# Four-layer graph network on one core: TensorE transposes the identity 6 to 20 times ahead of four of its waits

## The chip, the cores and the metric

One core of one Trainium2 chip runs the whole program. The metric is the device time of one execution in microseconds (us), and less is better. The program has five instruction streams that meet only at semaphores: TensorE (PE in the profile, PEld for its weight loads), VectorE (DVE), ScalarE (ACT), GpSimd (POOL) and SyncE (SP).

## The reference, cut to what matters

Sixteen graphs (batches) of 512 nodes with 256 features, each with its own 512x512 adjacency, go through four layers. After each layer the result is added to its input and normalized.

```python
x = _layernorm(x + _L0_gnn_ref(x, adj, ...))   # graph attention, one head, ELU
x = _layernorm(x + _L1_gnn_ref(x, adj, ...))   # three blocks: attention, layernorm, feed-forward 256-1024-256, layernorm
x = _layernorm(x + _L2_gnn_ref(x, adj, ...))   # graph attention that keeps the 16 largest weights of a row, ELU
x = _layernorm(x + _L3_gnn_ref(x, adj, ...))   # eight heads, relu, output projection
# one block of layer 1
scores = leaky(si[:, :, None] + sj[:, None, :] + attn_b[l]); attn = softmax(where(mask, scores, -inf))
h = layernorm(x + attn @ x, g1[l], beta1[l])
x = layernorm(h + gelu(h @ W1[l] + b1[l]) @ W2[l] + b2[l], g2[l], beta2[l])
```

Batches don't depend on each other. Everything is computed in float32.

## The kernel before

All weights stay in SBUF. Two batches are under way at any time, one in each of two slots with buffers of their own, half a batch apart: while one slot does the middle of its batch (layers L0, L1.0, L1.1 and the attention of L1.2), the other does the end of the batch before (the feed-forward of L1.2, then L2 and L3). The table HALF (line 56 on) is a hand-written order of named stages for one such pass, and every engine walks the same table, in the same order, doing its own part of each stage. A pass with one slot in the middle and a pass with the other in the middle alternate: an opening, seven turns of a loop of two passes, and a closing, so that each stage below runs 16 times in the program.

So an engine never overtakes within its own stream: if TensorE waits in a stage, all that stands behind it in HALF waits as well, whichever slot it belongs to.

PSUM has eight banks, four for each slot: `work` banks 0 and 1, which the slot's stages use in turn, and `acc` banks 0 and 1, in which the aggregations, the feed-forward's second product and the projections accumulate. The class `Use` (line 336) gives for the n-th use of a stage its bank, and the count that the bank's `evacuated` semaphore must have reached for the bank to be free. One stage's tile is in bank i % 2 of a running number i, so the tile after two transposed tiles takes the bank of the first of the two.

A stage's name has the layer beside it. Those around the change, as TensorE does them:

- `xT0`, `xT1`: wait until half of the rows is normalized (VectorE, line 732), and transpose it in two work tiles of two 128x128 transposes (line 1067). ScalarE copies the first tile to XT (line 911, for the h of the blocks line 972), VectorE the second (line 630, for h line 775).
- `v0` of L2 (line 1097): waits for both copies, then multiplies the half with the weights, in two work tiles.
- `s` and `bc` of L1.0 (lines 1110, 1126): attention scores of every node, 16 matmuls of two columns, and the spread of one of them by transposes.
- `pT0` to `pT3` (line 1138): wait for the exponential of a row tile, transpose the weights; `agg0`, `agg1` (line 1152): wait for the copies of the transposed weights (ScalarE line 950, VectorE line 711) and multiply them with the features.
- `hT0`, then `f100` (line 1174): the first feed-forward product of the first half, which waits for both copies of hT0's tiles; `f101` to `f103` are the rest of it, and `f200` (line 1188) begins the second product.

The wait in `f100` and what follows are these lines:

```python
if quarter == 0:
    for c in range(DC):
        u = Use(s, it, f"hT{half} {key}", c)
        pe.wait_ge(u.evacuated, u.turn + 1)
for f in range(quarter * FQ, (quarter + 1) * FQ):
    u = Use(s, it, f"g{half} {key}", f)
    pe.wait_ge(u.evacuated, u.turn)
```

In HALF the pieces stand so: `L1.2 f210 f211`, `L2 xT0`, `L0 norm1`, `L2 v0`, `L1.0 xT1 s bc`, `L1.2 f212 f213`, `L1.0 zs0 mx0 zs1 exp0 mx1 exp1 pT0`, `L1.0 pT1`, `L1.0 agg0`, `L1.0 pT2 pT3`, `L2 xT1 v1 bc`, `L2 zs0 mx0`, `L1.0 agg1`, `L2 zs1 exp0`, `L1.0 hT0 ha0 sum1 norm1 f100 f101 hT1 ha1`. In this list ScalarE has the exponentials (`exp0` of L2) ahead of its copy for `hT0`.

Of the kernel before, what the change touches and what calls it, by code (L numbers as in the profile page):

```python
# [12 lines left out]
P = 128  # L13
# [44 lines left out]
def build(nc, x, adj, w0, a01, a02, attn_w, attn_b, w1, b1, w2, b2, g1, beta1, g2, beta2,  # L58
# [81 lines left out]
    ]  # L140

    def half_batch(middle, other, after, ending=True, starting=True):
# [14 lines left out]
    with ExitStack() as ctx:  # L157
# [897 lines left out]
        def _(pe):  # L1055
            pe.wait_ge(consts, N_CONSTS)

            def wait_weights(key):
                pe.wait_ge(loaded[key], 16 * N_LOADS[key])
                pe.wait_ge(folded[key], N_FOLDED[key])  # L1060

            def transpose_tiles(s, it, key, src, row_tiles):
                for c in range(DC):
                    u = Use(s, it, key, c)
                    pe.wait_ge(u.evacuated, u.turn)
                    for i, t in enumerate(row_tiles):
                        last = pe.transpose(u.bank[:, i * P:(i + 1) * P], src[:, t, c * P:(c + 1) * P], ident[:])  # L1067
                    last.then_inc(u.filled, 1)

            def xT(half):  # L1070
                def stage(s, it, key):
                    if key == "L0":
                        pe.wait_ge(x_in.sems[s], x_in.value(it, "L0", 15))
                        transpose_tiles(s, it, "xT L0", HX[s], range(NT))
                    elif key in L1K[1:]:
                        pe.wait_ge(normed.sems[s], normed.value(it, L1K[L1K.index(key) - 1] + " x", half))
                        transpose_tiles(s, it, f"xT{half} {key}", HX[s], tiles(half))
                    else:
                        pe.wait_ge(normed.sems[s], normed.value(it, MADE_BY[key], half))
                        transpose_tiles(s, it, f"xT{half} {key}", X1[s], tiles(half))  # L1080
                return stage
# [6 lines left out]
            def project_v(half):  # L1088
                def stage(s, it, key):
                    weights, columns = {"L0": (w0_sb, DA), "L2": (wg_sb, DA), "L3": (wv_sb, D)}[key]  # L1090
                    if key != "L0" or half == 0:
                        wait_transposed(s, it, key, half)
                    for t in tiles(half):
# [35 lines left out]
            def weights_transposed(t):  # L1129
                def stage(s, it, key):  # L1130
                    if key == "L2":
                        pe.wait_ge(kept.sems[s], kept.value(it, key, t))
                    else:
                        pe.wait_ge(exp_done.sems[s], exp_done.value(it, key, t))
                    u = Use(s, it, f"pT {key}", t)
                    pe.wait_ge(u.evacuated, u.turn)
                    for j in range(NT):
# [4 lines left out]
            def agg(half):  # L1142
                def stage(s, it, key):
                    pe.wait_ge(acc_evacuated[half].sems[s], acc_evacuated[half].value(it, key) - 1)
                    src = SOURCE[key] if key in L1K else V
                    if key in L1K[1:] and half == 0:
# [10 lines left out]
            def h_transposed(half):  # L1157
                def stage(s, it, key):
                    pe.wait_ge(normed.sems[s], normed.value(it, key + " h", half))
                    transpose_tiles(s, it, f"hT{half} {key}", HX[s], tiles(half))  # L1160
                return stage

            def ffn1(half, quarter):
                def stage(s, it, key):
                    l = L1K.index(key)
                    if quarter == 0:
                        for c in range(DC):
                            u = Use(s, it, f"hT{half} {key}", c)
                            pe.wait_ge(u.evacuated, u.turn + 1)
# [157 lines left out]
```

## Time and profile before

| | before |
|---|---|
| median of 3 runs | 3887.73 us (3886.62 to 3899.89) |
| the profiled execution | 3898.82 us |
| its span, first to last instruction | 3896.9 us |
| mean granted TensorE clock | 0.946 of full |
| PE busy | 3453.9 us, 89% of the span, 18816 matmuls |
| DVE, ACT, POOL busy | 2408.7, 2204.8, 695.6 us (62%, 57%, 18%) |

Busy is the time in which an engine has an instruction in it; matmuls are pipelined, so that their starts lie closer than one lasts. The granted clock is the share of TensorE's 2.4 GHz that the chip let through: it has two levels, 1.00 (2.4 GHz) and 0.50 (1.2 GHz), and values between them are means over a stretch. An idle time has behind it the instruction whose end released it.

### The profile page before, as it was taken

The page shows a single profiled execution, that of the slowest core. Times are in us where ns is not written, and L with a number is a line of the kernel's source. Part 1 is how long each engine was busy: PE and PEld are TensorE (multiplying, and loading weights), DVE is VectorE, ACT ScalarE, POOL GpSimd, SP SyncE. Part 2 cuts the span into 40 slices and gives each one's busy share as a digit, 9 for nine tenths or more (in the row PEclk, how much of TensorE's full clock was granted, in tenths as well). Part 3 has the DMA queues.
Part 4 walks back from the last instruction along what each step waited for, and adds up shares of the span by engine and source line. Part 5 has one row for each costly group of instructions (what it writes and reads, how often), then busy time and mean ns, then how long its engine had stood idle before and what let it go on. Part 6 is the DMA issues. An engine that isn't in the chain of part 4 may idle for free.

```text
span 3896.9 us, 60670 instructions
## 1 busy us (share of the span) xinstructions
PE 3453.9 (89%) x18816; PEld 2690.3 (69%) x18816; DVE 2408.7 (62%) x6661; ACT 2204.8 (57%) x4383; POOL 695.6 (18%) x684
## 2 busy tenths in 40 slices
PE   6789989898998989989898898989989899898976
PEld 5667767767777677777777677677767777677653
DVE  3366676666657566676666756566666666766554
ACT  2256556565564746556575564746646565565633
POOL 1211121121212111121121211112121121211110
PEclk8799999999999999999999999999999999999988
DMA  5000000000000000000000000000000000000000
GB/s 129 0 1 12 7 12 7 6 6 6 12 7 6 6 6 12 7 12 6 1 12 7 12 7 6 7 7 12 6 12 7 1 12 6 12 7 1 1 6 6
DMA packets 42354, 39.73 MB, mean 10 GB/s; under 512 B 10017, under 2 KB 40993, under 8 KB 42017
## 3 DMA queue, kind: packets, MB, share of 16 engines
q1 hardware_dynamic: 33568, 27.17, 2.4%
q0 software_dynamic: 8448, 8.39, 1.5%
q8 instruction: 172, 2.82, 0.3%
q14 instruction: 166, 1.35, 0.1%
HBM read 35.55 MB, written 8.39 MB: 11 GB/s over the span
## 4 chain that ended last, share of the span: by engine, by line
PE 48%; issue 33%; DVE 8%; ACT 5%; POOL 5%; DVEq 0%; DMA 0%; POOLq 0%; ACTq 0%; SPq 0%
PE acc L1188 7%; PE work L1174 7%; PE acc L1152 6%; PE work L1097 4%; PE acc L1223 4%; PE acc L1254 3%; POOL rstd L503 3%; PE acc L1235 3%; PE work L1203 2%; PE acc L1283 2%; PE work L1067 2%; PE work L1110 2%; ACT PT L1000 2%; PE work L1235 2%; PE work L1138 1%
## 5 line engine op out<-in xcount | busy, mean ns | idle before, releaser
L1174 PE MATMUL work<-XT,w_sb 128*128 128x256 f32 x3072 | 740.6, 389 | 79.6 <-ACT XT L972 60.9
L503 POOL TENSOR_TENSOR rstd<-var_eps,minus_half 128x2 f32<-128x2 f32 x320 | 233.5, 730 | 3027.9 <-DVE var_eps L727 3027.9
L1188 PE MATMUL acc<-w_sb,gT 128*128 128x256 f32 x3072 | 741.3, 389 | 0.0
L1174 PEld LDWEIGHTS work<-XT,w_sb 128*128 128x128 f32 x3072 | 565.6, 192 | 215.5 <-issue 60.1
L1188 PEld LDWEIGHTS acc<-w_sb,gT 128*128 128x128 f32 x3072 | 588.4, 196 | 101.2 <-issue 22.8
L982 ACT ACTIVATE gT<-work,b_sb 128x256 f32<-128x256 f32 x768 | 346.4, 473 | 227.0 <-PE work L1174 222.5
L1152 PE MATMUL acc<-X,PT 128*128 128x256 f32 x1536 | 359.8, 388 | 32.0 <-ACT PT L950 31.3
L1152 PEld LDWEIGHTS acc<-X,PT 128*128 128x128 f32 x1536 | 292.1, 194 | 86.9 <-issue 48.5
L711 DVE COPY PT<-work 128x512 f32<-128x512 f32 x160 | 110.2, 688 | 237.4 <-PE work L1138 234.7
L718 DVE BATCH_NORM_STATS2 stats<-R 128x6 f32<-128x256 f32 x640 | 240.9, 418 | 11.0
L1152 PE MATMUL acc<-V,PT 128*128 128x256 f32 x1024 | 234.7, 382 | 4.0 <-ACT PT L950 3.8
L982 ACT ACT_TABLE_LOAD x183 | 234.8, 1283 | 3.2
L920 ACT ACTIVATE V<-work 128x258 f32<-128x258 f32 (+1 forms) x192 | 74.1, 386 | 282.5 <-PE work L1097 282.5
L651 DVE CUSTOM_DVE_ANT_0 T<-T,pos 128x512 f32<-128x512 f32 x256 | 178.8, 735 | 63.1 <-ACT T L928 63.1
L658 DVE SCALAR_TENSOR_TENSOR T<-T 128x512 f32<-128x512 f32 x320 | 217.2, 684 | 0.0
L1152 PEld LDWEIGHTS acc<-V,PT 128*128 128x128 f32 x1024 | 192.8, 191 | 31.6 <-issue 4.6
L942 ACT ACTIVATE T<-T,neg_max 128x512 f32<-128x512 f32 x256 | 182.2, 713 | 55.2 <-DVE neg_max L663 51.4
L950 ACT ACTIVATE PT<-work 128x512 f32<-128x512 f32 x160 | 94.7, 592 | 207.7 <-PE work L1138 207.7
L1138 PE MATMUL work<-ident,T 128*128 128x128 f32 x1280 | 176.8, 278 | 31.2 <-ACT T L942 18.4
L928 ACT ACTIVATE T<-work,s 128x512 f32<-128x512 f32 x192 | 117.9, 688 | 144.5 <-PE work L1126 144.5
L1138 PEld LDWEIGHTS work<-ident,T 128*128 128x128 f32 x1280 | 152.7, 143 | 62.5 <-ACT T L942 25.0
L1000 ACT ACTIVATE PT<-PT,head_min 128x512 f32<-128x512 f32 x256 | 182.7, 715 | 0.5
(146 smaller groups left out, 6015.0 us busy)
## 6 DMA issues: line engine op xcount, KB each, us to landing
HX<-in_x SPq DMA_DIRECT2D x16, 512.0 KB, 3.9
pos<-in_adj POOLq DMA_DIRECT2D x16, 512.0 KB, 5.5
out<-X SPq DMA_DIRECT2D x32, 256.0 KB, 2.1
w_sb<-in_L_gnn_W SPq DMA_DIRECT2D x6, 1024.0 KB, 7.9
g_sb<-in_L_gnn_g SPq DMA_DIRECT2D x6, 128.0 KB, 4.7
c_sb<-in_L_gnn_beta SPq DMA_DIRECT2D x3, 128.0 KB, 4.3
PT<-in_L_gnn_b SPq DMA_DIRECT2D x3, 128.0 KB, 5.5
beta_sb<-in_L_gnn_beta SPq DMA_DIRECT2D x1, 384.0 KB, 7.7
```

The costliest lines, as they stand in the source:

```text
L503: pool.tensor_tensor(rstd[s][:, half_rows(half)], var_eps[s][:, half_rows(half)], minus_half[:], ALU.pow)\
L651: dve.tensor_tensor_reduce(T[s][:, t, :], T[s][:, t, :], pos[s][:, t, :], 1.0, HIGHEST, ALU.add, ALU.min, neg_row[s][:, t:t + 1]).then_inc ...
L658: dve.scalar_tensor_tensor(T[s][:, t, :], T[s][:, t, :], ALPHA[key], T[s][:, t, :], ALU.mult, ALU.max if key == "L2" else ALU.min).then_in ...
L718: last = dve.bn_stats(stats[s][:, t, :], R[s][:, t, :])
L942: act.activation(to, T[s][:, t, :], ACT.Exp, bias=neg_max[s][:, t:t + 1], scale=1.0 if key == "L2" else -1.0, accum_out=den[s][:, t:t + 1] ...
L982: act.activation(gT[s][:, f, :], u.bank[:, 0:HN], ACT.Gelu, bias=b1_sb[:, l, f:f + 1]).then_inc(u.evacuated, 1)
L1000: act.activation(z, z, ACT.Exp, bias=head_min[s][:, n:n + 1], scale=-1.0, accum_out=den3[s][:, m, half * HT + i, r:r + 1]).then_inc(exp_do ...
L1138: last = pe.transpose(u.bank[:, j * P:(j + 1) * P], T[s][:, t, j * P:(j + 1) * P], ident[:])
L1152: last = pe.matmul(acc[s][half][:, t % HT, :], PT[s][:, j, t * P:(t + 1) * P], src[s][:, j, 0:D], start=(j == 0 and t % HT == 0), stop=(j ...
L1174: last = pe.matmul(u.bank[:, 0:HN], w1_sb[:, l, c, f * P:(f + 1) * P], XT[s][:, c, half * HN:(half + 1) * HN], start=(c == 0), stop=(c == ...
L1188: last = pe.matmul(acc[s][half][:, i, :], gT[s][:, f, i * P:(i + 1) * P], w2_sb[:, l, f, :], start=(f == 0 and i == 0), stop=(f == FC - 1) ...
L1235: last = pe.transpose(use.bank[:, j * P:(j + 1) * P], score_tile(s, n)[:, j * P:(j + 1) * P], ident[:])
```

## The change

A table FILLERS names four stages and a count for each. Ahead of them TensorE transposes the identity matrix that many times into columns 0 to 127 of the bank that the stage is about to fill; nothing reads the result, and the stage's first product overwrites the bank. Since a bank must be free before it is written, a wait for that comes ahead of the transposes. In `pT` stages, which are not in the table, the two waits change places.

```diff
+    FILLERS = {("L1.0", "f100"): 20, ("L2", "xT1"): 9, ("L1.0", "agg0"): 10, ("L2", "v0"): 6}
...
+            def fill_in(bank, stage, key):
+                for _ in range(FILLERS.get((key, stage), 0)):
+                    pe.transpose(bank[:, 0:P], ident[:], ident[:])
+
+            def fill_in_ahead(s, it, use, stage, key):
+                if (key, stage) in FILLERS:
+                    u = Use(s, it, use, 0)
+                    pe.wait_ge(u.evacuated, u.turn)
+                    fill_in(u.bank, stage, key)
+
...
                     else:
+                        fill_in_ahead(s, it, f"xT{half} {key}", f"xT{half}", key)
                         pe.wait_ge(normed.sems[s], normed.value(it, MADE_BY[key], half))
                         transpose_tiles(s, it, f"xT{half} {key}", X1[s], tiles(half))
...
                     if key != "L0" or half == 0:
+                        fill_in_ahead(s, it, "v L0" if key == "L0" else f"v{half} {key}", f"v{half}", key)
                         wait_transposed(s, it, key, half)
...
             def weights_transposed(t):
                 def stage(s, it, key):
+                    u = Use(s, it, f"pT {key}", t)
+                    pe.wait_ge(u.evacuated, u.turn)
+                    fill_in(u.bank, f"pT{t}", key)
                     if key == "L2":
                         pe.wait_ge(kept.sems[s], kept.value(it, key, t))
                     else:
                         pe.wait_ge(exp_done.sems[s], exp_done.value(it, key, t))
-                    u = Use(s, it, f"pT {key}", t)
-                    pe.wait_ge(u.evacuated, u.turn)
...
             def agg(half):
                 def stage(s, it, key):
                     pe.wait_ge(acc_evacuated[half].sems[s], acc_evacuated[half].value(it, key) - 1)
+                    fill_in(flat(acc[s][half]), f"agg{half}", key)
...
                     if quarter == 0:
+                        fill_in_ahead(s, it, f"g{half} {key}", f"f1{half}0", key)
                         for c in range(DC):
                             u = Use(s, it, f"hT{half} {key}", c)
                             pe.wait_ge(u.evacuated, u.turn + 1)
```

`fill_in_ahead` is also called in `h_transposed` and for the later blocks' `xT`, where the table has no entry and it does nothing.

TensorE's stream from `L1.0 hT0` to `L1.0 f100` in the first loop pass, before. Names carry slot and bank: work_1_1 is slot 1's work bank 1; brackets hold the semaphores waited for.

```order
L1067 MATMUL work_1_1<-ident,HX_1 128x128 [waits evacuated_1_1,normed_1]
L1067 MATMUL work_1_1<-ident,HX_1 128x128
L1067 MATMUL work_1_0<-ident,HX_1 128x128 [waits evacuated_1_0]
L1067 MATMUL work_1_0<-ident,HX_1 128x128
L1169 REGISTER_ALU [waits evacuated_1_1]
L1174 MATMUL work_1_1<-XT_1,w1_sb 128x256 [waits evacuated_1_1,evacuated_1_0]
L1174 MATMUL work_1_1<-XT_1,w1_sb 128x256
```

The same piece with the change:

```order
L1081 MATMUL work_1_1<-ident,HX_1 128x128 [waits evacuated_1_1,normed_1]
L1081 MATMUL work_1_1<-ident,HX_1 128x128
L1081 MATMUL work_1_0<-ident,HX_1 128x128 [waits evacuated_1_0]
L1081 MATMUL work_1_0<-ident,HX_1 128x128
L1068 MATMUL work_1_1<-ident 128x128 [waits evacuated_1_1]
L1068 MATMUL work_1_1<-ident 128x128 x19
L1190 REGISTER_ALU [waits evacuated_1_1]
L1195 MATMUL work_1_1<-XT_1,w1_sb 128x256 [waits evacuated_1_1,evacuated_1_0]
L1195 MATMUL work_1_1<-XT_1,w1_sb 128x256
```

The 20 new transposes stand between hT0's transposes and f100's first product, behind a wait for bank work_1_1, into which hT0's first tile has just been written.

TensorE's stream at `L1.0 agg0`, then `pT2`, `pT3` and `L2 xT1`, in the same pass with the change:

```order
L1068 MATMUL acc_1_0<-ident 128x128 [waits acc_evacuated0_1]
L1068 MATMUL acc_1_0<-ident 128x128 x9
L1171 MATMUL acc_1_0<-X1_1,PT_1 128x256 [waits evacuated_1_1]
L1171 MATMUL acc_1_0<-X1_1,PT_1 128x256 x3
...
L1156 MATMUL work_1_0<-ident,T_1 128x128 x3
L1068 MATMUL work_0_1<-ident 128x128 [waits evacuated_0_1]
L1068 MATMUL work_0_1<-ident 128x128 x8
L1095 REGISTER_ALU
L1081 MATMUL work_0_1<-ident,X1_0 128x128 [waits evacuated_0_1,normed_0]
```

Here the new transposes wait for a bank alone, and the stage's own wait (for the copied weights, evacuated_1_1, or for the normalized rows, normed_0) comes behind them. Before, `agg0` waited for both at once, and `xT1` for evacuated_0_1 and normed_0.

## Rows read from the trace of the kernel before

**Rows 1.** The page: busy time, and granted clock in 40 slices of the span.

```profile
PE 3453.9 (89%) x18816; PEld 2690.3 (69%) x18816; DVE 2408.7 (62%) x6661; ACT 2204.8 (57%) x4383; POOL 695.6 (18%) x684
...
PEclk8799999999999999999999999999999999999988
```

**Rows 2.** Waits of PE: engine, line <- releaser: us in total, times, longest us.

```profile
PE work L1174 <- ACT XT L972: 60.9, 45, 3.3
PE work L1067 <- DVE X L732: 48.5, 34, 7.9
PE work L1097 <- DVE XT L630: 41.1, 33, 2.3
PE acc L1152 <- ACT PT L950: 35.2, 24, 2.4
PE work L1138 <- ACT T L942: 18.4, 5, 5.1
```

**Rows 3.** Timeline, L1.0 hT0 to f100: start us, us, engine line op [idle before <-releaser].

```profile
1683.48 0.60 PE L1067 MATMUL work<-ident,HX 128*128 128x128 f32 x4
...
1685.67 0.53 DVE L775 TENSOR_SCALAR XT<-work,g1t_sb,beta1t_sb 128x256 f32<-128x256 f32 x1
...
1686.57 0.55 ACT L972 ACTIVATE XT<-work,beta1t_sb,g1t_sb 128x256 f32<-128x256 f32 x1
...
1687.35 1.19 PE L1174 MATMUL work<-XT,w_sb 128*128 128x256 f32 x2 [3.27 <-ACT XT L972]
```

**Rows 4.** Timeline of PE alone: transposes at full clock.

```profile
3854.77 1.04 PE L1235 MATMUL work<-ident,T 128*128 128x128 f32 x8
```

**Rows 5.** Windows, f100 to f200: stretch, length, busy by engine, PEclk, DMA share, GB/s.

```profile
750.29:758.56 8.27, 7.90 (x37) 6.29 (x37) 5.12 (x19) 4.84 (x9) 3.24 (x3) 1.00 0.00 0
981.77:992.80 11.03, 10.67 (x36) 8.42 (x37) 5.12 (x19) 4.84 (x9) 3.23 (x3) 0.75 0.00 1
```

**Rows 6.** Windows, L1.0 f200 to L1.1 xT1, behind the two stretches of rows 5.

```profile
758.56:796.25 37.69, 36.57 (x173) 29.84 (x172) 27.11 (x61) 19.13 (x34) 5.87 (x7) 1.00 0.05 15
992.80:1030.50 37.70, 36.58 (x174) 29.85 (x172) 27.19 (x61) 19.13 (x34) 5.88 (x7) 1.00 0.05 15
```

**Rows 7.** Timeline, L2 xT0 to v0.

```profile
714.98 0.60 PE L1067 MATMUL work<-ident,X 128*128 128x128 f32 x4
...
715.40 0.38 ACT L911 ACTIVATE XT<-work 128x256 f32<-128x256 f32 x1 [0.86 <-PE work L1067]
...
717.02 0.42 DVE L630 COPY XT<-work 128x256 f32<-128x256 f32 x1
...
717.50 1.49 PE L1097 MATMUL work<-wg_sb,XT 128*128 128x258 f32 x3 [1.92 <-DVE XT L630]
```

**Rows 8.** Windows, L2 v0 to L1.2 f212 (v0, xT1, s, bc), three passes.

```profile
1656.29:1661.81 5.52, 4.85 (x33) 4.28 (x33) 1.33 (x4) 1.05 (x3) 0.36 (x1) 1.00 0.01 3
1887.98:1894.98 7.00, 6.53 (x33) 5.39 (x34) 1.33 (x4) 1.16 (x3) 0.00 (x0) 0.76 0.00 1
1419.51:1427.73 8.22, 7.82 (x32) 6.85 (x33) 1.33 (x4) 1.16 (x3) 0.00 (x1) 0.58 0.00 1
```

**Rows 9.** Windows, L1.2 f212 to L1.0 agg0.

```profile
1661.81:1669.68 7.87, 4.92 (x26) 3.72 (x25) 6.61 (x20) 5.94 (x13) 0.00 (x0) 1.00 0.00 0
724.74:732.66 7.92, 6.08 (x25) 4.96 (x25) 6.61 (x20) 5.94 (x13) 0.00 (x0) 0.80 0.00 0
```

**Rows 10.** Timeline, L1.0 agg0 and L2 xT1.

```profile
732.66 3.69 PE L1152 MATMUL acc<-X,PT 128*128 128x256 f32 x16 [1.84 <-ACT PT L950]
...
738.81 0.66 PE L1067 MATMUL work<-ident,X 128*128 128x128 f32 x4 [1.59 <-DVE X L732]
```

**Rows 11.** Windows, L1.1 xT1 to L1.1 agg0, three passes.

```profile
1734.89:1748.13 13.24, 11.70 (x66) 7.27 (x65) 10.41 (x30) 7.79 (x18) 5.59 (x4) 1.00 0.27 41
1969.14:1983.71 14.57, 13.16 (x65) 8.51 (x65) 10.51 (x30) 7.79 (x18) 5.59 (x4) 0.88 0.27 38
1263.74:1279.39 15.65, 14.62 (x65) 9.57 (x65) 10.67 (x30) 7.79 (x18) 5.59 (x4) 0.78 0.24 35
```

**Rows 12.** Windows: two stretches at the granted clock 1.00, each with the one behind it.

```profile
3854.60:3858.00 3.40, 1.84 (x16) 1.39 (x13) 1.34 (x2) 3.03 (x8) 0.00 (x0) 1.00 0.00 0
3858.00:3874.00 16.00, 10.72 (x96) 6.82 (x97) 8.27 (x23) 10.13 (x27) 0.00 (x0) 1.00 0.00 1
414.00:417.30 3.30, 3.30 (x23) 2.37 (x21) 0.17 (x1) 1.04 (x2) 0.00 (x0) 1.00 0.00 0
417.40:424.10 6.70, 5.55 (x28) 3.45 (x32) 6.16 (x18) 5.01 (x12) 0.00 (x0) 0.50 0.00 0
```

**Rows 13.** Windows, L1.2 xT1 to L1.2 agg0 (s, bc, L3 proj0 in it).

```profile
1816.62:1834.85 18.23, 16.97 (x106) 11.46 (x105) 11.29 (x32) 10.48 (x23) 2.54 (x2) 0.81 0.00 1
```

More of the change, by code:

```diff
@@ L1078, in stage @@
                     else:
+                        fill_in_ahead(s, it, f"xT{half} {key}", f"xT{half}", key)
                         pe.wait_ge(normed.sems[s], normed.value(it, MADE_BY[key], half))
@@ L1158, in stage @@
                 def stage(s, it, key):
+                    fill_in_ahead(s, it, f"hT{half} {key}", f"hT{half}", key)
                     pe.wait_ge(normed.sems[s], normed.value(it, key + " h", half))
```

## The prediction

> **What bounds the kernel now.** The page comes first [rows 1]: PE has an instruction in it for 3453.9 of 3896.9 us, 89%, and no other engine is over 62%. The kernel is bound by TensorE's stream, with some 440 us in which PE waits, and by its clock: the mean granted clock is 0.946, and since it has only the levels 1.00 and 0.50, some 420 us of the span ran at half clock (0.054 x 3896.9 / 0.5). The list of PE's waits is second [rows 2]. Its four longest entries are 60.9, 48.5, 41.1 and 35.2 us, and they contain the four waits that the change touches. Third, the timeline and the windows of single passes tell what each wait is, and what clock and time follow it.
>
> A pass is about 235 us and there are 16 of each stage, so that 1 us on PE's path in one stage is 16 us of the total. 0.5% of the time, about what a measurement can tell from no change, is 19.4 us.
>
> **What a delay of PE is worth.** The trace holds the test. The stretch from f100 to f200 takes 8.27 us at full clock and 11.03 us when the clock is down to 0.75 in it [rows 5], with the same work. The stretch behind it takes 37.69 us after the short one and 37.70 us after the long one [rows 6]. So the later waits don't give such a delay back. I take delays there in full.
>
> **Cost of one new transpose.** Eight transposes at full clock last 1.04 us from the first start to the last end [rows 4]. One alone lasts some 0.28 us (the four of hT0 take 0.60 [rows 3], so (0.60 - 0.28) / 3 = 0.11), and so they start every (1.04 - 0.28) / 7 = 0.109 us. At half clock I take twice that, 0.22.
>
> **f100, 20 transposes.** This is the largest wait, 3.27 us [rows 3], and the transposes don't stand in it. They are written into the bank of hT0's first tile, and that tile is emptied by ScalarE's copy, L972. It begins at 1686.57 and lasts 0.55; VectorE's copy of the second tile, L775, ended at 1686.20. f100 starts at 1687.35, released by the same L972. So the wait that the transposes need is the one that f100 has today, and they run behind it, on PE's path: 20 x 0.109 = 2.2 us, x 16 = **+34.9 us**. Queued behind them are f100 itself, f101 and hT1, for whose tile ScalarE and VectorE then wait; by [rows 5, 6] it isn't won back. Bounds: 0 if all of it were absorbed later, and 16 x 20 x 0.22 = 70 us if all ran at half clock. I take full clock, since 11 of the 16 such stretches [rows 5] read 1.00.
>
> **v0 of L2, 6 transposes.** Their bank is emptied by ScalarE's L911, 715.40 + 0.38 = 715.78, and v0 starts at 717.50, released by VectorE's L630 [rows 7]. 6 x 0.109 = 0.65 us fit into these 1.7 us, also at half clock (1.3). Cost 0, hidden by VectorE's statistics ahead of L630; with that cover gone 0.65 x 16 = 10 us.
>
> **agg0 of L1.0, 10 transposes,** and **xT1 of L2, 9.** Here the new work really stands ahead of the wait. Their banks were emptied stages earlier, and 1.1 us goes into a wait of 1.84 us for the copied weights, 1.0 us into one of 1.59 us for the normalized rows [rows 10]. Cost 0; one of the passes has no wait at xT1, and there it is 1.0 us.
>
> **One more wait** for a bank in each place, with its register work: four a batch at 0.05 us, **+3 us** (0 to 6).
>
> **What the clock gives back.** It can only be read where it fell.
> The stretch from L2 v0 to L1.2 f212 takes 5.52 us at 1.00, 7.00 at 0.76, 8.22 at 0.58 [rows 8]. Of 15 passes five are near the first (5.5 to 5.9), seven near the second, three near the third; over 5.5 us they sum to 19.5 us. The long PE idle in front of these falls is v0's 1.92 us, and 0.65 us of transposes now stand in it. The very next stages stream little (s has matmuls of two columns), so that I don't count on all: two thirds, **-13 us** (0 to -19.5).
> The stretch from f212 to agg0 reads 0.80 in 14 of 15 passes, and costs nothing: 7.92 us at 0.80, 7.87 at 1.00, because agg0 waits for ScalarE anyway [rows 9]. What the transposes ahead of agg0 do for the clock there is worth 0.
> Behind f100 five of 16 stretches fell; over 8.27 us they sum to 11.6 us. The transposes leave the idle 3.27 us as it is, and take the place of matmuls behind it. I take 0, from -11.6 to +30 (the other eleven at 2.76 us each).
> The stretch from L1.1 xT1 to agg0 has no transposes, but costs 13.24, 14.57 or 15.65 us by its clock [rows 11], three, four and eight of 15 passes, 24 us in sum over the shortest. What decides is when PE arrives, which the change moves by 2 us a pass. I take 0, from -24 to +12.
>
> **Do transposes hold the clock?** 16 transposes in a stretch of 3.40 us, with PE busy for 1.84 us and with no other matmul, leave the clock at 1.00, also in the 16 us behind [rows 12]. On the other hand PE is busy for all of 3.30 us in the stretch before 417.30, with two-column matmuls and ones of four rows, and the clock is 0.50 in the next 6.70 us. So by these rows a transpose counts much like a matmul, and what does not count are operations that stream little. The Trainium skill, page TensorE: Matmul & The Clock Gate, section Part 4: PE-mode transpose, says that the full clock does not engage for transposes, since they don't count as a busy PE. By that rule this change could not hold the clock at all: the sum would be +38 us, against the +25 us that the rows give. It is a rival below.
>
> **Sum:** 34.9 + 3 - 13 = +25 us. Against the profiled execution (3898.8) that is 3924; against the median of the runs, 11 us lower at 3887.73, it is 3913, +0.65%.
>
> **The rivals.**
> *A, the clock comes back in more places: faster.* If the falls in [rows 8, 11] and behind f100 all went, that would be 19.5 + 24 + 11.6 = 55 us. The stretch around L3 proj0 reads 0.81 in all 16 passes [rows 13]: 6.8 us at half clock. A later arrival could shorten it, at most 3.4 us x 16 = 54. The change is faster from the point where more than 38 of these 109 us go. With the first 55 and a tenth of the rest, 3887.7 + 38 - 55 - 5 = 3866. For it: which passes fell is a matter of arrival, as passes with the same work show. Against it: three of the four places get no new work where PE idles.
> *B, the delay is half absorbed: no change.* PE waits for VectorE and ScalarE after f100 too. If these waits took half of 35 us, 3887.7 + 17 + 3 - 13 = 3895. Against it: the windows behind f100 [rows 6], which show 0.01 us given back of 2.76.
> *C, transposes don't hold the clock,* the rule just named, with no gain beside v0: 3887.7 + 38 = 3926. Against it: the 16 transposes of [rows 12].
> *D, f100 falls more often.* The idle 3.27 us is followed by 20 transposes and not by matmuls. If the clock is down behind it in all passes, 3913 + 30 = 3943.
> *The change doesn't do what it says* is not a rival of its own: at f100 that is my forecast, since there it stands behind the wait.
>
> **How the numbers follow.** Forecast 0.38, with 0.07 of it under 3907; A 0.14, B 0.25, C 0.10, D 0.13. Slower by over 0.5%: 0.31 + 0.10 + 0.13 = 0.54. Within 0.5%: 0.25 + 0.07 = 0.32. Faster: 0.14. The range reaches from A's value to D's, 3867 to 3943, and leaves out the outer halves of both.
>
> **What the profile of the changed kernel would show.** The new transposes as 16 x 45 = 720 instructions on a line of their own. PE's wait at f100 for ACT L972 stays near 3.27 us, with its waiter now the new transposes, and f100's first matmul comes 2.2 us after their first. The wait for L630 ahead of v0 shrinks from 1.92 to about 1.1 us, that for L950 from 1.84 to 0.7, that for L732 from 1.59 to 0.6. The windows from v0 to f212 are at 5.5 us in most passes, f200 to L1.1 xT1 stays at 37.7. The forecast is wrong if the transposes at f100 begin before L972 ends, if 37.7 becomes shorter by about 2 us, or if the windows of [rows 11, 13] move to a higher clock in most passes.

## The result, and the profile after

| | before | with the change |
|---|---|---|
| median of the runs (lowest to highest) | 3890.34 us (3886.62 to 3899.89, 4 runs) | 3924.13 us (3922.06 to 3927.24, 4 runs) |
| ratio, 95% interval | | 1.0084 [1.0063, 1.0104] |
| profiled execution, its span | 3898.82, 3896.9 us | 3925.57, 3923.6 us |
| mean granted clock | 0.946 | 0.956 |

The change makes the kernel slower by 0.84%, some 34 us (25 to 40 by the interval). The profiled execution of before lay 8 us above its median, so that the two spans differ by 27 us only.

The page after, to be read against [rows 1]: busy time, and granted clock in 40 slices.

```profile
PE 3513.5 (90%) x19536; PEld 2752.3 (70%) x19536; DVE 2407.3 (61%) x6661; ACT 2202.6 (56%) x4383; POOL 695.4 (18%) x684
PEclk8799999999999999999999999999999999999988
```

PE has 19536 - 18816 = 720 more instructions, 16 x 45. The mean clock rose by 0.010 and the time rose with it.

The waits of PE after, against [rows 2] (engine, line <- releaser: us in total, times, longest us). L976, L736, L954 and L634 are L972, L732, L950 and L630 of before.

```profile
PE work L1068 <- ACT XT L976: 46.7, 16, 3.1
PE work L1081 <- DVE X L736: 35.2, 35, 6.9
PE acc L1171 <- ACT PT L954: 23.6, 23, 2.0
PE work L1114 <- DVE XT L634: 22.7, 31, 1.2
```

The groups of the new line L1068 (out<-in xcount | busy, mean ns of one | idle before them, and its releasers):

```profile
L1068 PE MATMUL work<-ident 128*128 128x128 f32 x560 | 93.5, 333 | 50.8 <-ACT XT L976 46.7 <-ACT XT L915 4.1
L1068 PE MATMUL acc<-ident 128*128 128x128 f32 x160 | 20.6, 277 | 0.0
```

Three waits became shorter: xT1's from 48.5 to 35.2 us (with other stages of that line in it), agg0's from 35.2 to 23.6, v0's from 41.1 to 22.7. The fourth only changed its waiter: the new transposes now sit idle for 46.7 us, 16 times up to 3.1 us, until ScalarE's copy ends. The two groups differ in what one transpose lasts: 277 ns ahead of agg0, 333 ns on the work banks, where f100's 320 are. They ran partly at half clock, as the timeline from hT0 to f100 shows (start us, us, engine line op [idle before <-releaser]), against [rows 3]:

```profile
1928.51 0.60 PE L1081 MATMUL work<-ident,HX 128*128 128x128 f32 x4
...
1931.61 0.55 ACT L976 ACTIVATE XT<-work,beta1t_sb,g1t_sb 128x256 f32<-128x256 f32 x1
1932.20 4.07 PE L1068 MATMUL work<-ident 128*128 128x128 f32 x20 [3.09 <-ACT XT L976]
1936.11 1.68 PE L1195 MATMUL work<-XT,w_sb 128*128 128x256 f32 x7
```

L976 ends at 1932.16 and the transposes begin at 1932.20. f100 starts 3.91 us behind their start, where it could have started itself at 1932.20. At full clock 20 of them would have needed 2.2 us. The window of these 3.91 us reads 0.56, nearly all of it half clock:

```profile
1932.20:1936.11 3.91, 3.90 (x20) 3.91 (x21) 1.77 (x7) 1.25 (x1) 1.76 (x2) 0.56 0.02 4
```

At v0, then at agg0 and xT1, against [rows 7, 10]:

```profile
1898.97 0.38 ACT L915 ACTIVATE XT<-work 128x256 f32<-128x256 f32 x1 [0.86 <-PE work L1081]
1899.41 0.87 PE L1068 MATMUL work<-ident 128*128 128x128 f32 x6 [0.26 <-ACT XT L915]
1900.98 0.42 DVE L634 COPY XT<-work 128x256 f32<-128x256 f32 x1 [0.30 <-issue]
1901.46 1.36 PE L1114 MATMUL work<-wg_sb,XT 128*128 128x258 f32 x5 [1.18 <-DVE XT L634]
...
1912.20 1.26 PE L1068 MATMUL acc<-ident 128*128 128x128 f32 x10
1914.75 3.72 PE L1171 MATMUL acc<-X,PT 128*128 128x256 f32 x16 [1.29 <-ACT PT L954]
1919.18 1.15 PE L1068 MATMUL work<-ident 128*128 128x128 f32 x9
1920.91 0.66 PE L1081 MATMUL work<-ident,X 128*128 128x128 f32 x4 [0.59 <-DVE X L736]
```

In these three places the transposes have ended 0.6 to 1.3 us before the wait ends. They stand in it and delay nothing.

The windows of one pass (stretch, length, busy by PE, PEld, DVE, ACT and POOL, granted clock, DMA share, GB/s): L2 v0 to L1.2 f212 [rows 8], f100 to f200 [rows 5], L1.0 f200 to L1.1 xT1 [rows 6], L1.1 xT1 to agg0 [rows 11], and the stretch with L3 proj0 [rows 13].

```profile
1901.46:1906.98 5.52, 4.86 (x33) 4.29 (x33) 1.33 (x4) 1.05 (x3) 0.00 (x0) 1.00 0.01 1
1936.11:1944.31 8.20, 7.83 (x39) 6.22 (x38) 3.54 (x12) 3.77 (x8) 1.47 (x2) 1.00 0.00 1
1944.31:1982.00 37.69, 36.58 (x173) 29.85 (x172) 27.17 (x61) 19.11 (x34) 5.88 (x7) 1.00 0.04 15
1982.00:1996.70 14.70, 13.28 (x66) 8.37 (x65) 10.50 (x30) 7.79 (x18) 5.59 (x4) 0.88 0.26 37
2065.20:2083.42 18.22, 16.97 (x106) 11.45 (x105) 11.28 (x32) 10.53 (x23) 2.55 (x2) 0.81 0.01 2
```

**Where the time went.** The 14 middle passes of the loop were cut at the starts of their stages, in every kernel's profiled execution. Each figure is the sum of a stretch over the 14 passes in us, and behind the stroke how much of it ran at half clock (length x (1 - clock) / 0.5); an empty place or a missing second figure was not summed:

| stretch | before | no_entries | change | no_f100 | f100_free_bank |
|---|---|---|---|---|---|
| pass start to f200 | 171.5 / 6.3 | 171.6 / 6.5 | 176.8 / 16.6 | 169.9 | 172.0 |
| v0 to f212 | 96.8 / 45.4 | 87.5 / 23.6 | 78.2 / 2.9 | 80.2 / 6.9 | 78.6 / 3.9 |
| f212 to agg0 | 110.5 / 43.3 | 110.4 / 41.2 | 108.9 / 10.8 | 109.2 / 27.2 | 109.0 / 13.2 |
| agg0 to f100's first product | 246.3 / 7.3 | 246.9 / 17.1 | 297.3 / 44.3 | 247.6 | 247.7 / 0 |
| f100 to f200 | 127.3 / 23.4 | 127.6 / 23.9 | 116.5 / 3.5 | 134.3 / 37.5 | 115.8 / 0 |
| f200 to L1.1 xT1 | 527.8 | 527.8 | 527.7 | | |
| L1.1 xT1 to agg0 | 209.4 / 68.3 | 209.6 / 71.7 | 207.5 / 47.8 | 209.9 / 71.7 | 206.0 / 47.8 |
| L1.2 xT1 to agg0 | 258.2 / 95.6 | 258.6 / 95.6 | 255.4 / 95.6 | 258.8 | 256.5 / 95.6 |
| all 14 passes | 3290.1 | 3283.6 | 3311.3 | 3284.5 | 3256.0 |

The other three stretches (f200 to v0 in two parts, and L1.1 agg0 to L1.2 xT1) and the end of the pass differ by 1 us or less between before and the change. The change gains 18.6 us at v0, 10.8 behind f100 and 6.3 at three others, loses 51.0 ahead of f100 and 5.3 at the pass start: +21 us. Another 6.3 us come up behind the loop, and 0.8 is gained ahead of it, which makes the 27 us of the spans.

The column no_entries is the changed code without any transpose, an experiment further down whose time is that of before. Each column is one execution, and these two, both without transposes, differ at v0: 96.8 us in one, 87.5 in the other. So what the transposes gain at v0 is 9 to 19 us in 14 passes, depending on which of the two it is measured from. The 51 us ahead of f100 don't depend on it (246.3 and 246.9). Behind f100 the two agree in time (127.3 and 127.6), but 5 of the 14 passes fell in one and 7 in the other. Whether this is chance between executions or the changed order of two waits was not tested.

### The profile page after: what moved, and what is told of

It is laid out like the page before. It is cut to its first block, busy times and chain, and to the rows that moved or that the text cites. A ratio compares the mean times of both kernels' runs of the same rounds, so it can differ in the third digit from the quotient of the medians.

```text
span 3923.6 us, 61877 instructions
## 1 busy us (share of the span) xinstructions
PE 3513.5 (90%) x19536; PEld 2752.3 (70%) x19536; DVE 2407.3 (61%) x6661; ACT 2202.6 (56%) x4383; POOL 695.4 (18%) x684
## 4 chain that ended last, share of the span: by engine, by line
PE 46%; issue 35%; DVE 7%; ACT 5%; POOL 5%; DVEq 0%; DMA 0%; POOLq 0%; ACTq 0%; SPq 0%
PE acc L1209 7%; PE work L1195 7%; PE acc L1171 6%; PE work L1114 5%; PE acc L1244 4%; PE acc L1275 3%; POOL rstd L507 3%; PE acc L1256 3%; PE acc L1304 2%; PE work L1081 2%; PE work L1224 2%; ACT PT L1004 2%; PE work L1256 2%; PE work L1127 2%; ACT T L932 1%
## 5 line engine op out<-in xcount | busy, mean ns | idle before, releaser
L1195 PE MATMUL work<-XT,w_sb 128*128 128x256 f32 x3072 | 730.1, 385 | 30.4 <-ACT gT L986 14.6
L1209 PE MATMUL acc<-w_sb,gT 128*128 128x256 f32 x3072 | 724.8, 383 | 0.0
L1209 PEld LDWEIGHTS acc<-w_sb,gT 128*128 128x128 f32 x3072 | 576.5, 192 | 96.3 <-issue 22.8
L1171 PE MATMUL acc<-X,PT 128*128 128x256 f32 x1536 | 356.2, 386 | 21.7 <-ACT PT L954 19.9
L954 ACT ACTIVATE PT<-work 128x512 f32<-128x512 f32 x160 | 94.6, 591 | 197.6 <-PE work L1156 197.2
L932 ACT ACTIVATE T<-work,s 128x512 f32<-128x512 f32 x192 | 117.7, 687 | 134.3 <-PE work L1143 134.3
```

Of the source, the lines that this page charges most:

```text
L1171: last = pe.matmul(acc[s][half][:, t % HT, :], PT[s][:, j, t * P:(t + 1) * P], src[s][:, j, 0:D], start=(j == 0 and t % HT == 0), stop=(j ...
L1195: last = pe.matmul(u.bank[:, 0:HN], w1_sb[:, l, c, f * P:(f + 1) * P], XT[s][:, c, half * HN:(half + 1) * HN], start=(c == 0), stop=(c == ...
L1209: last = pe.matmul(acc[s][half][:, i, :], gT[s][:, f, i * P:(i + 1) * P], w2_sb[:, l, f, :], start=(f == 0 and i == 0), stop=(f == FC - 1) ...
```

## Theories, and the experiments

Three theories went to the chip.
- **S** (the prediction's): the transposes ahead of f100 stand behind ScalarE's copy, on PE's path, and cost their full time; those ahead of v0 stand in a wait and hold the clock; those at agg0 and xT1 are hidden and worth nothing. What counts for the clock is how much PE streams.
- **W**: it is the code around them that costs, the added waits and the changed order of the two waits in `pT`.
- **T**: transposes don't hold the clock, and what v0 gains comes from another arrival time of PE.

The runs were in three comparisons with a kernel before of its own: 3895.75 us (3888.74 to 3904.05), 3896.29 (3890.44 to 3904.53) and 3897.61 (3886.84 to 3905.17). Kernels of different comparisons are compared by their ratios.

| label | median, us | ratio to before, 95% interval | clock |
|---|---|---|---|
| no_f100 | 3885.84 | 0.9976 [0.9966, 0.9986] | 0.952 |
| f100_free_bank | 3866.19 | 0.9925 [0.9908, 0.9941] | 0.962 |
| v0_narrow | 3899.47 | 1.0007 [0.9997, 1.0017] | 0.946 |
| v0_only | 3886.54 | 0.9977 [0.9967, 0.9987] | 0.950 |
| f100_only | 3932.89 | 1.0092 [1.0075, 1.0109] | 0.944 |
| f100_free_narrow | 3889.66 | 0.9984 [0.9974, 0.9994] | 0.955 |
| rb1_14 | 3882.32 | 0.9963 [0.9950, 0.9975] | 0.965 |
| rb1_14_s_6 | 3915.94 | 1.0054 [1.0036, 1.0073] | 0.961 |
| no_entries | 3895.75 | 0.9996 [0.9982, 1.0009] | 0.948 |
| free_f100_v0 | 3870.70 | 0.9924 [0.9896, 0.9953] | 0.954 |
| f100_10 | 3899.95 | 1.0008 [0.9996, 1.0020] | 0.957 |
| rt1_10_rb1_14 | 3884.86 | 0.9973 [0.9961, 0.9985] | 0.975 |

### no_entries: the code alone

```diff
-    FILLERS = {("L1.0", "f100"): 20, ("L2", "xT1"): 9, ("L1.0", "agg0"): 10, ("L2", "v0"): 6}
+    FILLERS = {}
```

> The changed code with an empty FILLERS: only the changed order of the two waits in pT is left, and no transpose. S: the time of before, 3890 to 3898. W (waits and order carry part of the loss): 3905 or more.

Measured: 0.9996 [0.9982, 1.0009]. What remains is the changed order of the waits in `pT`, and it costs nothing that can be measured (the interval reaches from -7 to +4 us). W falls, as far as that order goes; the wait ahead of each filled stage is only made with an entry, and is in the runs below.

### no_f100: without f100's entry

```diff
+    FILLERS = {("L2", "xT1"): 9, ("L1.0", "agg0"): 10, ("L2", "v0"): 6}
```

> FILLERS without the entry for f100. Theory S (the transposes at f100 stand behind ScalarE's copy, on PE's path, and those ahead of v0 hold the clock): 54 us go with the 20 transposes, and 11 us of falls behind f100 return; from 3924 that is some 3870 (3860 to 3880), faster than before; the stretch from agg0 to f100's first product is back at 17.6 us, v0 to f212 stays at 5.5. Theory W (the loss is the added waits and the changed order of waits in pT, the same in all places): 3905 to 3920. Theory T (transposes don't hold the clock; 5.5 us beside v0 was a matter of arrival): about 3890, with v0 to f212 back at 5.5 to 8.2 us.

Measured: 0.9976. Against the change's 1.0084 the one entry costs 42 us (0.0108 x 3890). The other three entries with all their waits are a gain, which ends W altogether. But S wanted more of them, 3860 to 3880 us, and by its time alone this run would fit T (about 3890). The profile shows the v0 stretch as expected and the stretch behind f100 (second row) worse than in the change:

```profile
1887.29:1893.22 5.93, 5.26 (x32) 4.70 (x33) 1.33 (x4) 1.05 (x3) 0.00 (x0) 0.92 0.00 1
1918.68:1928.64 9.96, 9.59 (x36) 7.58 (x37) 5.12 (x19) 4.84 (x9) 3.23 (x3) 0.83 0.00 1
```

Before, 5 of the 16 stretches behind f100 fell to the half clock. Here it is 11 of 14, each at some 10 us. So 7 of the 17 us gained at v0 against before's profile are given back there, and 4.5 more at the end of the pass, a stretch that the table leaves out (163.2 us against 158.7).

### f100_only: only f100's entry

```diff
+    FILLERS = {("L1.0", "f100"): 20}
```

> Only the entry for f100, 20 transposes behind ScalarE's copy as in the change. S: agg0 to f100's first product 21.2 us as in the changed kernel, f100 to f200 8.2 to 8.5; v0 to f212 back to 6.8 in the mean. 3892 + 53 - 11 = 3934 (3922 to 3946), the slowest of all. Theory W (waits and order): no more than 3905.

Measured: 1.0092 [1.0075, 1.0109], the slowest of all. The stretch ahead of f100 grew from 246.3 to 290.7 us in the 14 passes (47.2 at half clock), v0 to f212 stayed at 94.9, and f100 to f200 went down to 120.1. The loss is this entry's, without the others. The run also parts the two terms of its cost, in two passes from agg0 to f100's first product:

```profile
736.69:756.38 19.69, 14.01 (x81) 11.81 (x81) 15.80 (x47) 7.45 (x14) 5.63 (x6) 1.00 0.00 1
971.55:993.25 21.70, 16.09 (x80) 13.90 (x81) 16.42 (x48) 7.45 (x14) 7.02 (x8) 0.88 0.00 1
```

Five of its 14 passes stayed at 1.00 and took 19.60 to 19.70 us, 2.1 more than before. The nine with a fall took 20.7 to 21.7.

### f100_10: half as many at f100

```diff
+    FILLERS = {("L1.0", "f100"): 10, ("L2", "xT1"): 9, ("L1.0", "agg0"): 10, ("L2", "v0"): 6}
```

> The changed kernel with 10 in place of 20 transposes at f100, still behind ScalarE's copy. S: the cost goes with their number, from the kernel without the entry (3886) to the change (3924): 3905 (3895 to 3914). agg0 to f100's first product 1.1 us over 17.6 at full clock and 2.2 at half.

Measured: 1.0008, 3899.95 us. Against no_f100 the ten cost 12 us (0.0032), against 42 for twenty. In the profile the stretch ahead of f100 is 266.8 us, 1.4 us a pass longer than in no_f100, at half clock for 12.0 us in the 14 passes (44.3 with twenty). Ten last 1.09 us at full clock, twenty should last 2.2 and took 3.6: the cost grows faster than the number, because the later transposes meet the half clock. In this run the stretch L1.1 xT1 to agg0, where nothing was put in, also became shorter, 196.5 us against 209.4 before, with 8 of 14 passes at 1.00 instead of 2. So falls do come and go far behind the filled places.

### f100_free_bank: the same 20, into a bank that is free

The transposes now go into the accumulator bank of this half, which f200 fills later. Their wait is for the evacuation of agg0's result, which was in that bank before and left it long ago.

```diff
-                        fill_in_ahead(s, it, f"g{half} {key}", f"f1{half}0", key)
+                        if (key, f"f1{half}0") in FILLERS:
+                            pe.wait_ge(acc_evacuated[half].sems[s], acc_evacuated[half].value(it, key + " ffn") - 1)
+                            fill_in(flat(acc[s][half]), f"f1{half}0", key)
```

> All four entries, but the 20 transposes at f100 are written into acc bank 0, which the second product fills later and which is free already, so that they stand ahead of the copy's wait. S: they go into the idle 3.27 us (20 x 0.109 = 2.2), f100 starts 17.6 us after agg0, its clock stays at 1.00, f100 to f200 is 8.2 us in all passes: 3858 (3848 to 3872), better than without them by the 11 us of falls. W: as the changed kernel, 3915 to 3925. T: no better than without the entry for f100.

Measured: 3866.19 us, 0.9925 [0.9908, 0.9941]. The number and the shape of the transposes are the change's. Only the bank is another one, and with it the wait, and the kernel is 1.6% faster than the change. The timeline of hT0 to f100:

```profile
1898.67 0.60 PE L1081 MATMUL work<-ident,HX 128*128 128x128 f32 x4
1899.11 2.35 PE L1068 MATMUL acc<-ident 128*128 128x128 f32 x20
1901.77 0.55 ACT L976 ACTIVATE XT<-work,beta1t_sb,g1t_sb 128x256 f32<-128x256 f32 x1
1902.55 1.32 PE L1197 MATMUL work<-XT,w_sb 128*128 128x256 f32 x5 [1.09 <-ACT XT L976]
```

The transposes begin right behind hT0's, last 2.35 us, and end before ScalarE's copy begins. f100 starts at the end of that copy, as in [rows 3], after an idle time of 1.09 us and not 3.27. The window from there to f200:

```profile
1902.55:1910.82 8.27, 7.90 (x36) 6.29 (x37) 5.11 (x19) 4.83 (x9) 3.23 (x3) 1.00 0.01 3
```

All 14 passes read 8.27 us at 1.00. The wait list says the same of all 16 passes, where PE waited 60.9 us in [rows 2] for this copy:

```profile
PE work L1197 <- ACT XT L976: 28.3, 45, 1.1
```

### f100_free_narrow: the same time in matmuls of two columns

In f100_free_bank's code the 20 transposes are replaced by nine products of the identity with two of its columns, each of which shows as two matmuls:

```diff
-                            fill_in(flat(acc[s][half]), f"f1{half}0", key)
+                            for _ in range(9):
+                                pe.matmul(flat(acc[s][half])[:, 0:2], ident[:], ident[:, 0:2], start=True, stop=True)
```

> As the kernel with the free bank, but at f100 9 matmuls of two columns (18 instructions, some 2 us) stand in the wait in place of the 20 transposes; the other three entries are transposes. S with its part that streaming counts: f100 to f200 is at 10 us with the clock under 1.00 in half of the passes or more, as without an entry there, time 3885 (3876 to 3895). Rival (PE must only be busy): f100 to f200 at 8.2 in all, 3866.

Measured: 0.9984 [0.9974, 0.9994]. The timeline shows them in the same gap, and then the window from f100 to f200:

```profile
1908.93 2.07 PE L1190 MATMUL acc<-ident 128*128 128x2 f32 x18
...
1912.37 2.16 PE L1198 MATMUL work<-XT,w_sb 128*128 128x256 f32 x5 [1.37 <-ACT XT L976]
```

```profile
1912.37:1922.32 9.95, 9.59 (x36) 7.57 (x37) 5.10 (x19) 4.83 (x9) 3.23 (x3) 0.83 0.01 2
```

PE was busy for 2.07 us here and for 2.35 with the transposes. The clock fell behind f100 in 13 of 14 passes here and in none there. With nothing in the gap (no_f100) it fell in 11 of 14, and the time was 0.9976: the narrow products did nothing for the clock. PE reached f100 equally late in both runs (247.9 and 247.7 us from agg0), so the arrival is not the cause, and an instruction in PE is not enough. The pair is not matched to the last: PE idles 1.37 us behind the narrow products and 1.09 behind the transposes. The next pair is matched more closely. T falls, and the Trainium skill's sentence that transposes don't count (page TensorE: Matmul & The Clock Gate, section Part 4: PE-mode transpose) does not hold for these transposes: by it these two runs should have fallen alike.

### v0_only and v0_narrow: the same question at v0

```diff
+    FILLERS = {("L2", "v0"): 6}
```

> Only the entry for v0, 6 transposes. S: v0 to f212 5.5 us in nearly all passes against 6.8 in the mean before, -18 us, time 3872 (3862 to 3884); the entries for agg0 and xT1 are worth nothing, so that this equals the kernel without the f100 entry within 8 us. T: 3890 (3884 to 3900), v0 to f212 6.8 in the mean.

Measured: 0.9977 [0.9967, 0.9987]. The first row is v0 to f212, the second f100 to f200.

```profile
1882.43:1887.95 5.52, 4.85 (x32) 4.29 (x33) 1.33 (x4) 1.05 (x3) 0.00 (x0) 1.00 0.00 1
1913.48:1923.44 9.96, 9.59 (x37) 7.54 (x37) 5.12 (x19) 4.83 (x9) 3.23 (x3) 0.83 0.00 1
```

v0 to f212 falls from 96.8 (no_entries: 87.5) to 78.4 us, the whole gain that the change has there. But f100 to f200 rises from 127.3 (127.6) to 137.4: 13 of 14 passes now fall behind f100. The six transposes alone do at v0 what the four entries do, and half of it or all of it, by which kernel one compares with, is lost some stages on. The time, 3886.5 us, lies above S's range (to 3884) and in T's; only the windows part the two.

v0_narrow puts three products of two columns (six matmuls, 0.83 us) in their place:

```diff
+    FILLERS = {("L2", "v0"): 3}
...
-                    fill_in(u.bank, stage, key)
+                    for _ in range(FILLERS[key, stage]):
+                        pe.matmul(u.bank[:, 0:2], ident[:], ident[:, 0:2], start=True, stop=True)
```

> Only one entry, v0, and there 3 matmuls of the identity with two of its columns (6 instructions, some 0.7 us) in place of 6 transposes. S, with the part that what counts for the clock is what is streamed, not that PE is busy: v0 to f212 as before, 5.5 to 8.2 us and 6.8 in the mean, time 3890 (3880 to 3900). Rival (any work in the wait holds the clock): v0 to f212 at 5.5 in nearly all, time as with the 6 transposes, some 3872.

Measured: 1.0007 [0.9997, 1.0017], the time of before. v0 to f212 took 84.9 us with 18.3 at half clock. That is less than the 96.8 / 45.4 of before, but about what no_entries has with nothing in the wait (87.5 / 23.6), so that it shows no effect of the narrow products. The six transposes last as long (0.87 against 0.83 us) and leave the same idle time behind them (1.18 against 1.23 us), and with them the stretch reads 78.4 / 2.7. Over all the runs the ten kernels with the six transposes took 77.2 to 80.3 us there, at half clock for 7.8 or less, and the four without them 84.9 to 96.8 us, with 18.3 to 45.4. This too speaks against T.

### free_f100_v0: are agg0 and xT1 worth anything?

f100_free_bank's code with two entries:

```diff
+    FILLERS = {("L1.0", "f100"): 20, ("L2", "v0"): 6}
```

> The kernel with the free bank without the entries for agg0 and xT1; only f100 (free bank) and v0 are left. S: falls between f212 and agg0 cost nothing, so that agg0's and xT1's transposes are worth nothing: 3866 within 6 us, f100 to f200 8.2 in all. Rival (the transposes ahead of agg0 and xT1 each keep a fall away that costs): 3876 or more.

Measured: 0.9924 [0.9896, 0.9953], against 0.9925 with all four. The 19 transposes at agg0 and xT1 cost nothing and bring nothing that this run can show (its interval is 11 us to either side): f212 to agg0 is 110.3 us here and 109.0 there, and the 41.0 us of half clock between agg0 and f100 that their absence leaves (0 there) cost no time, 247.4 against 247.7 us.

### rb1_14, rb1_14_s_6, rt1_10_rb1_14: the stretch around L3 proj0

This stretch reads 0.81 or 0.82 in all 14 passes of before [rows 13]. It holds products of two columns (s) and of four rows (rb0, rb1), and a wait ahead of proj0. On top of f100_free_bank, 14 transposes were put ahead of rb1, then 6 more ahead of each s of L1.1, then 10 ahead of rt1 with the 14 of rb1, each behind the wait that the stage has for its bank.

```diff
+    FILLERS = {("L1.0", "f100"): 20, ("L2", "xT1"): 9, ("L1.0", "agg0"): 10, ("L2", "v0"): 6, ("L3", "rb1"): 14}
...
+                    fill_in(use.bank, f"rb{m}", key)
```

> The kernel with the free bank and 14 transposes more ahead of L3 rb1, between the two-column matmuls of L1.2 s and the four-row matmuls of rb1, where PE does not wait and the clock falls in every pass. S: they cost 14 x 0.109 = 1.5 us of PE a pass and keep the clock, which costs 3.4 us a pass there: L1.2 xT1 to agg0 from 18.3 to 16.4 us, 3866 - 30 = 3836 (3826 to 3850). T (transposes don't hold the clock): 14 x 0.22 = 3 us more in each pass, 3866 + 49 = 3915.

```diff
+    FILLERS = {..., ("L3", "rb1"): 14, ("L1.1", "s"): 6}
...
+                fill_in(u.bank, "s", key)
```

> As the last, and 6 transposes ahead of L1.1 s (0.65 us a pass), where the clock fell in most passes for 1.3 to 2.4 us. S: L1.1 xT1 to agg0 from 14.7 in the mean to 13.9, 3836 - 12 = 3824 (3814 to 3842). T: 3915 + 10.

```diff
+    FILLERS = {..., ("L3", "rt1"): 10, ("L3", "rb1"): 14}
...
+                    fill_in(use.bank, f"rt{m}", key)
```

> As the kernel with 14 ahead of rb1, which fell to half clock in the two-column matmuls ahead of the 14, and 10 transposes more ahead of rt1, in front of those matmuls. S: now the clock holds through s and rb1; cost 24 x 0.109 = 2.6 us a pass against 3.4 won: L1.2 xT1 to agg0 at 17.5 to 18, 3866 - 10 = 3856 (3846 to 3872). If the clock falls in spite of them, the transposes are a cost alone: 3890 or more.

Measured, against f100_free_bank's 0.9925: 0.9963, 1.0054 and 0.9973. All three are misses, of 29 us and more. The timeline of rb1_14 in one pass, and then the window of its whole stretch:

```profile
1579.40 1.84 PE L1127 MATMUL work<-aw_sb,XT 128*128 128x2 f32 x16
...
1581.10 2.44 PE L1068 MATMUL work<-ident 128*128 128x128 f32 x14
...
1583.47 2.07 PE L1299 MATMUL work<-T,head_rows 4*128 4x512 f32 x2
```

```profile
1574.64:1596.08 21.44, 20.18 (x120) 13.80 (x119) 11.29 (x32) 10.53 (x23) 2.55 (x2) 0.76 0.01 2
```

Two pieces of that pass, s alone and then the transposes:

```profile
1579.40:1581.10 1.70, 1.70 (x18) 1.70 (x17) 0.00 (x0) 0.59 (x1) 0.00 (x0) 1.00 0.00 0
1581.10:1583.47 2.37, 2.37 (x16) 2.04 (x15) 0.17 (x1) 0.00 (x0) 0.00 (x0) 0.68 0.00 0
```

The clock fell among the transposes, although PE was busy all the time, right behind 1.70 us of products of two columns. I read it as the fall that those products bring on, which the 14 came too late to prevent. They had no idle time to stand in and cost their own 1.5 us, and in four of the 14 passes the half clock lasted 10.2 us where it had been 6.8 (in the ten others 3.4). The stretch went from 256.5 us in f100_free_bank to 276.4. With 6 more at s it went to 297.9 (136.5 at half clock), and L1.1 xT1 to agg0, where the six stand, from 206.0 to 213.1.

rt1_10_rb1_14 did what was meant for the clock. First the whole stretch of f100_free_bank, then its two parts up to proj0 and behind proj0's start, with the wait ahead of proj0 between them:

```profile
2031.56:2050.15 18.59, 16.87 (x107) 11.46 (x106) 11.20 (x32) 10.51 (x23) 2.55 (x2) 0.82 0.01 2
...
2031.56:2040.96 9.40, 7.68 (x51) 5.25 (x49) 3.82 (x9) 5.58 (x12) 2.55 (x2) 0.94 0.00 0
...
2039.80:2040.96 1.16, 0.00 (x1) 0.00 (x1) 1.08 (x3) 1.16 (x3) 0.00 (x0) 0.51 0.00 0
2040.96:2050.15 9.19, 9.19 (x57) 6.22 (x58) 7.38 (x24) 4.93 (x12) 0.00 (x0) 0.69 0.02 4
```

The same of rt1_10_rb1_14:

```profile
2039.92:2059.35 19.43, 17.13 (x130) 12.66 (x129) 10.93 (x31) 10.39 (x23) 2.55 (x2) 1.00 0.01 2
...
2039.92:2052.05 12.13, 10.42 (x74) 7.81 (x72) 3.81 (x9) 5.57 (x12) 2.55 (x2) 1.00 0.01 1
2052.05:2059.35 7.30, 6.71 (x56) 4.86 (x57) 7.12 (x23) 4.82 (x12) 0.00 (x0) 1.00 0.01 2
```

The clock is 1.00 in 12 of 14 passes, the half-clock time of the stretch fell from 95.6 to 6.8 us in the 14, and the kernel's mean clock is 0.975, the highest of any run. Yet the stretch is 0.84 us longer in this pass, and 1.2 a pass over the 14 (273.4 against 256.5 us). The 24 transposes put proj0's start 2.73 us later (24 x 0.109 = 2.6), and the full clock gave back 1.89 us behind it. Half of the 6.7 us of half clock would have been 3.4. It isn't had in full: 1.1 us of them lay in the wait ahead of proj0, where PE has nothing to do (0.51 over the 1.16 us), and behind proj0 PE now arrives early and waits for VectorE. This row of rt1_10_rb1_14's timeline stands where f100_free_bank has no wait:

```profile
2057.52 1.99 PE L1308 MATMUL acc<-wo_sb,XT 128*128 128x256 f32 x8 [0.59 <-DVE XT L865]
```

## Why the prediction was right, and where its sizes were off

It said 3913 us, slower by 0.65%, and it measured 3924, slower by 0.84%. The mechanism is the one that it named. The number alone would not show it: rival C, without any hold on the clock, said 3926. It is the windows at v0 and the pair of runs at f100 that exclude C. The steps:

- **f100's transposes stand on PE's path: right, shown.** Their wait is ScalarE's copy (46.7 us, 16 times), and with another bank, and nothing else changed, the loss turns into a gain.
- **Their size: the term that was mis-sized.** "I take full clock", +34.9 us. The stretch ahead of f100 grew by 51.0 us in 14 passes, 3.64 a pass or 58 for 16. The clock was down for 44.3 us there, 37.0 more than before, which adds half of that, 18.5, to the 14 x 2.18 = 30.5 us at full clock: 49 of the 51. f100_only shows the first part by itself: 2.1 us in each pass that stayed at full clock. The idle time of 3.1 us ahead of them stayed, and the fall that follows it came in every pass. The reading "11 of the 16 read 1.00" was of stretches behind f100 in which matmuls followed the idle time.
- **Behind f100: "I take 0, from -11.6".** The fall had been spent on the transposes, and f100 to f200 lost 10.8 us in the 14 passes. Rival D saw that the clock would fall in all passes, but put the fall on the matmuls, at +30; it fell on the transposes.
- **A delay at f100 is not won back: right.** f200 to L1.1 xT1 took 527.7 us against 527.8 in the 14 passes.
- **v0: -13 predicted, -18.6 measured in 14 passes** (some -21 for 16) against before's profile, and -9.3 (some -11) against that of no_entries. Twelve of 14 passes read 5.52 us, so that hardly any falls are left: the discount of a third for the stages that stream little was not needed. What was uncertain is how much there was to gain. The wait went from 1.92 to 1.18 us (said: 1.1).
- **agg0 and xT1: right,** hidden (waits 1.29 and 0.59 us remain; said 0.7 and 0.6) and worth nothing that shows, by free_f100_v0. The stretch f212 to agg0 lost 32.5 us of half clock and 1.6 us of time.
- **The added waits, +3 us:** not seen. L2 xT0 to v0, where v0's stands, took 37.9 us in 14 passes against 38.0; with xT1's alone (no_f100) agg0 to f100 took 247.6 against 246.3 or 246.9; at f100 at most 2 us are left unexplained. At agg0 no wait was added: the aggregation had it before.
- **L1.1 xT1 to agg0 and proj0: "I take 0".** -1.9 and -2.8 us. Rival A's shift by arrival hardly came in the time. But the sign that the prediction gave for it did: from L1.1 xT1 to agg0 the clock rose in 8 of 14 passes, from 0.78 to 0.88 or 0.89, stayed there in four and fell from 1.00 in two. That this made only 1.9 us was not foreseen. (Around proj0 the prediction's "0.81 in all 16 passes" is 15 of them: the first takes 14.18 us and reads 0.50.)
- **Not foreseen:** +5.3 us from the pass start to f200, all of it half clock (6.3 to 16.6, half of which is 5.2), and +6.3 us behind the loop. Over the kernels tried that first stretch took 169.9 to 176.8 us, with and without f100's entry, so that no entry is its cause as far as these runs tell.

Two errors offset: the transposes cost some 23 us more than taken, and v0 and the stretch behind f100 gave back some 20 more (some 10, measured from no_entries). That the total came so near is in part luck.

## What to carry to other kernels

Work that is put into a wait must itself be free to start: look up the semaphore that it needs, above all for the bank that it writes. A bank that was just filled comes free only with the very copy that the stage waits for. 20 transposes in that bank cost 42 us here, and in a bank long free they gained.

Here such work paid at the two waits where PE really idled ahead of a stage full of wide products, and where PE had no idle time it cost more than it gave back. And judge it by the time, not by the clock: by their ratios the two kernels with the highest mean clocks (0.975 and 0.965) are 19 and 15 us slower than the one with 0.962.

## What the hardware showed unexpectedly

- **A fall of the clock can be moved instead of removed.** v0_only took 18 us of falls away at v0 (9, measured from no_entries), and 10 came back behind f100, where the passes with a fall went from 5 of 14 (7 of 14 in no_entries) to 13 of 14, at the same 3.3 us of idle time. no_f100 shows the same with 11 of 14. Why the idle time is followed by a fall in these passes and in only a third to a half of them without any transposes was not settled: no run changed the moment of PE's arrival alone.
- **So the second gap was worth more than its own falls.** v0 filled alone gives 0.9977, both gaps 0.9924 or 0.9925: 21 us more for a stretch whose falls summed to 11.6 us in [rows 5]. f100_free_bank, 3866 us, beats the kernel before by 0.75% and is the best version found.
- **Products of two columns didn't hold the clock, though PE was nearly as long busy with them** (13 of 14 passes fell behind 2.07 us of them, none behind 2.35 us of transposes; at v0 0.83 us of them left 18.3 us of half clock, 0.87 us of transposes 2.7).
